# Two input chunk loads issued ahead of the constants, and the epilogue's f loads moved from GpSimd's queue to SyncE's

## The reference

```python
x = x + layernorm(attn(layernorm(x)))      # attn: LN, in_proj to 96, conv 3, silu,
                                           # selective scan (16 states), out_proj, + residual
x = x + layernorm(ffn(layernorm(x)))
def ffn(z):                                # router weight from a softmax over the top 2 of 8
    shared = (silu(z @ sh_gate.T) * (z @ sh_up.T)) @ sh_down.T      # 8192 wide
    routed = (silu(z @ r_gate.T) * (z @ r_up.T)) @ r_down.T         # 1024 wide
    return shared + routed * comb_w
```

## Time and profile before

| | |
|---|---|
| time, median of 3 runs | 2701.47 us (2700.31 to 2702.14) |
| the profiled execution's own time | 2702.35 us |
| its span (slowest core, core 7) | 2700.8 us |
| spans of the eight cores | 2684.7 to 2700.8 us |
| first TensorE instruction, core 7 | 24.83 us after the start |
| epilogue loop, from its first e1 to the end | 2569.16 to 2700.8 us |

### The profile page before, as it was taken

One profiled execution on the slowest core, in us unless ns is written; L12 is line 12 of the kernel. 1 busy time (PEld: TensorE's weight loads), 2 busy tenths in 40 slices (PEclk: granted clock), 3 DMA queues, 4 the chain that ended last, 5 costly groups with the idle time before them and its releaser, 6 DMA issues.

```text
span 2700.8 us, 27068 instructions; the slowest of 8 cores (2684.7 to 2700.8 us)
## 1 busy us (share of the span) xinstructions
PE 1921.2 (71%) x7719; PEld 779.8 (29%) x7719; DVE 396.1 (15%) x589; ACT 465.8 (17%) x802; POOL 363.7 (13%) x416
## 2 busy tenths in 40 slices
PE   4444543443323986899999999999979888888700
PEld 2111110000001432344444444444433333333300
DVE  0553343232363100000000000000000000000023
ACT  3333221231311112111111111111100000000100
POOL 1000000020200210122222222222200000000033
PEclk8655555555556989899999999999989999999855
DMA  6420001021132336444444444444434444344255
GB/s 100 59 32 0 0 0 62 1 78 48 44 121 55 63 67 152 78 79 78 77 74 74 75 78 79 79 79 78 76 66 92 94 94 90 84 92 94 55 187 179
DMA packets 67530, 203.23 MB, mean 75 GB/s; under 512 B 7420, under 2 KB 17789, under 8 KB 63302
## 3 DMA queue, kind: packets, MB, share of 16 engines
q0 software_dynamic: 40912, 132.88, 27.8%
q10 hardware_dynamic: 16128, 46.14, 4.6%
q1 hardware_dynamic: 10358, 22.48, 2.5%
HBM read 292.41 MB, written 33.55 MB: 121 GB/s over the span
## 4 chain that ended last, share of the span: by engine, by line
PE 66%; DVE 11%; DMA 8%; issue 7%; ACT 4%; POOL 2%; DVEq 0%; ACTq 0%; POOLq 0%; SPq 0%
PE pb L1120 16%; PE pb L1129 16%; PE pb L1174 5%; PE pb L1177 5%; PE pb L1189 4%; PE pb L1192 4%; DMA s_epf<-f_stash 2%; PE pb L1035 2%; PE pb L1044 2%; DVE s_xs L734 2%; PE pb L745 2%; DMA s_rdbuf<-Wrd 2%; POOL s_mr L858 2%; PE pb L1077 1%; DMA s_xhalf<-xT 1%
## 5 line engine op out<-in xcount | busy, mean ns | idle before, releaser
L1120 PE MATMUL pb<-s_z,s_gbuf 128*128 128x512 bf16 x2048 | 465.3, 380 | 13.6 <-issue 13.6
L1129 PE MATMUL pb<-s_z,s_ubuf 128*128 128x512 bf16 x2048 | 462.9, 379 | 0.0
L1120 PEld LDWEIGHTS pb<-s_z,s_gbuf 128*128 128x128 bf16 x2048 | 200.9, 98 | 257.4 <-issue 17.4
L1129 PEld LDWEIGHTS pb<-s_z,s_ubuf 128*128 128x128 bf16 x2048 | 200.4, 98 | 241.6
L1206 DVE TENSOR_TENSOR s_fstg<-pb,s_frbuf 128x512 f32<-128x512 f32 x32 | 20.6, 686 | 1545.2 <-PE pb L1192 1545.2
L1141 POOL TENSOR_TENSOR s_h<-s_gs,s_us 128x512 bf16<-128x512 bf16 x128 | 147.0, 1149 | 679.4 <-ACT s_us L1138 679.4
L1174 PE MATMUL pb<-s_h,s_dbuf 128*128 128x512 bf16 x512 | 209.6, 409 | 17.0 <-issue 16.6
L1177 PE MATMUL pb<-s_h,s_dbuf 128*128 128x512 bf16 x512 | 208.6, 407 | 0.0
L1189 PE MATMUL pb<-s_h,s_dbuf 128*128 128x512 bf16 x512 | 194.0, 379 | 4.1 <-PE pb L1177 4.1
L1192 PE MATMUL pb<-s_h,s_dbuf 128*128 128x512 bf16 x512 | 194.0, 379 | 0.0
L1135 ACT ACTIVATE s_gs<-pb 128x512 bf16<-128x512 f32 x128 | 76.4, 597 | 379.6 <-PE pb L1120 360.5
(11 more groups left out here) (193 smaller groups left out, 1479.9 us busy)
## 6 DMA issues: line engine op xcount, KB each, us to landing
s_gbuf<-Wg POOLq DMA_DIRECT2D x64, 512.0 KB, 5.2
s_ubuf<-Wu POOLq DMA_DIRECT2D x64, 512.0 KB, 7.1
s_dbuf<-Wd POOLq DMA_DIRECT2D x32, 1024.0 KB, 8.6
s_xcb<-xT POOLq DMA_DIRECT2D x5, 2048.0 KB, 18.1
s_xhalf<-xT SPq DMA_DIRECT2D x2, 4096.0 KB, 17.0
x_stash<-s_x2t ACTq DMA_DIRECT2D x32, 256.0 KB, 2.1
fr_stash<-s_frstg ACTq DMA_DIRECT2D x16, 512.0 KB, 5.4
s_frbuf<-fr_stash ACTq DMA_DIRECT2D x16, 512.0 KB, 7.7
```

The source lines that it names most:

```text
L1120: i2 = e.matmul(pb[bg][:, :], gbuf[ib][:, 128 * k:128 * (k + 1)], z4_sb[:, 1024 * k + hof:1024 * k + hof + 512], start=(k == 0), stop=(k = ...
L1129: i2 = e.matmul(pb[bu][:, :], ubuf[ib][:, 128 * k:128 * (k + 1)], z4_sb[:, 1024 * k + hof:1024 * k + hof + 512], start=(k == 0), stop=(k = ...
```

## The change

Two edits. `load_chunk` is defined earlier, and chunks 0 and 1 are issued by POOL ahead of its seven constants instead of behind them; the semaphores are dealt out anew by the rotation. In the epilogue, the f load is issued by SyncE instead of POOL, at the same place of the text, so that SyncE's list becomes f load 0, store 0, f load 1, store 1, and so on.

```diff
@@ prologue, behind the 16 loads of SyncE
+    x3 = xT.rearrange("(k p) t -> p k t", p=128)
+    t_xbf = [None] * NCHUNK
+    r_xcb_l = r_xcb
+
+    def load_chunk(c):
+        cc = c % 2
+        dst = xcb[cc].rearrange("p (k t) -> p k t", t=512)
+        t_xbf[c] = S.dma("gpsimd",
+                         lambda e, d=dst, c=c: e.dma_start(out=d,
+                                                           in_=x3[:, :, 512 * c:512 * (c + 1)]),
+                         writes=[r_xcb_l[cc]])
+
+    load_chunk(0)
+    load_chunk(1)
     for dst, src in [(outTbf, outT_h), (xprojTbf, xprojT_h), (dtprojTbf, dtprojT_h),
                      (selDbf, selD_h), (selBbf, selB_h), (selCbf, selC_h),
                      (routerTbf, routerT_h)]:
@@ mixer: the same lines removed here
-    load_chunk(0)
-    load_chunk(1)
@@ epilogue loop
-        t_lf = S.dma("gpsimd", lambda e, k=k, kk=kk: e.dma_start(
+        t_lf = S.dma("sync", lambda e, k=k, kk=kk: e.dma_start(
                          out=ep_f[kk][:], in_=f_st[k]), writes=[r_epf[kk]],
                      waits=[r_fst[k]])
```

## The result

The change made the kernel slower: 2768.47 us median against 2701.8 us, a ratio of 1.0247 (95% interval 1.0234 to 1.0259), or +66.7 us. The forecast was 2785 us, +83, in a range of 2748 to 2808. The profiled execution took 2766.97 us, its slowest core (core 2) spans 2765.4.

What follows compares the result with a forecast made beforehand. Only prologue (constants' consumers set the pace) and epilogue loop (a chain of waits) counted, the middle passing delays on. 2702.35 + 20.8 + 63.0 = 2786.2, median 0.9 lower: 2785 us predicted, 8-in-10 range 2748 to 2808.

Steps and rivals of the forecast that it cites:

- The prologue, +20.8: Kernel start: POOL's constants wait behind both chunk loads, so their consumers start at 45.6 us instead of 24.83.
- T1: Prologue: the time at which chunk 1 lands, put at 36.95 us.
- the rest behind it: Prologue after chunk 1: outT lands at 41.55, selB then routerT are issued, routerT lands 3.0 later, at 45.6 us.
- SyncE's constants cost nothing: Prologue: SyncE's 16 constants, in rounds of four, end at 33 us, before POOL's, so they add nothing.
- The f load leaves 5.69 us after e1: Epilogue loop: issued behind e3 and the store, the f load leaves 5.69 us after e1 instead of 3.67.
- It lands in 6.5: Epilogue loop: starting together with store and x2 load, the f load takes 6.5 us to land.
- the forecast's 63.0: Epilogue loop: 15 turns of 12.36 us instead of 8.16, +63.0 us.
- Rival A: Epilogue loop: f lands in about 4.5 us, not held by the store; turn 10.36, total 2755 us; chance 0.13.
- The tail at 0: Loop's end: the last e3 and store are as before, adding 0.
- Rival B: Prologue costs nothing: POOL's constants slip between the chunks' packets, only the loop is paid; 2764 us; chance 0.06.
- Rival C: Epilogue loop: SyncE's f loads run ahead of waiting stores, turn 5.2 us, -44; total 2678 us; chance 0.04.
- Rival D: Epilogue loop: SyncE's first byte comes sooner than GpSimd's, 0.6 against 1 us, 6 us lower; faster overall: chance under 0.01.

Runs made afterwards that it cites:

- edit-1 run: The kernel before with only chunks 0 and 1 moved ahead of POOL's constants, the f load left on POOL: 2724.02 us, ratio 1.0085.
- run without rotation: Chunks first, f load left on POOL; against that kernel, POOL's nine first DMAs got own semaphores, later instructions dropped waits for POOL's constants: 2679.7 us.
- e3: Not a run: the DVE instruction in each turn of the epilogue loop that the turn's store waits for; it takes 1.23 us.

## Why the prediction was right, and where its sizes were off

The sign and the mechanisms were right, the range held the time; one term was too large.

- *The prologue, +20.8.* Measured +21.4 on the mean of the cores, with the gaps and the order that were foretold. T1 was put at 36.95 and came at 39.2 to 42.2; the rest behind it was put at 8.7 us and took 5.8 to 6.8. Two errors that cancel: routerT took 2.0 and outT landed 1.4 us behind chunk 1, not 4.6. The edit-1 run confirms the whole, and the run without rotation shows that the semaphore waits, on which half of the argument rested, are 2 us of it. The order in POOL's queue, the other half, is the cause.
- *SyncE's constants cost nothing:* right. cconsts was issued at 24.77 on core 2 and landed 6.8 us later, and the last to land was routerT.
- *The f load leaves 5.69 us after e1:* 5.70 in the turn shown. Right.
- *It lands in 6.5:* this is the step that was mis-sized. I took the median of the store before and supposed that three transfers starting together would need the 7.5 us that they needed when one led. They needed 5.7, and f landed in 5.1 on core 2, 5.3 over all. 1.2 x 15 = 18 of the 19 us between the forecast's 63.0 and the 44.2 measured. The rows could not tell, since none had all three starting at once, but the trace before could have told more. At the start of its loop ACT issues the x2 loads of tiles 0, 1 and 2 within 0.9 us (2570.2 to 2571.1 on core 7), three 512 KB loads in one queue, and they land in

```profile
DMA to landing us min/median/max: 3.5/4.7/5.5
```

So the third, behind two others, takes 5.5 us and not 6.5. Rival A read the 3.5 of the first as that of a load that ran alone; it had two behind it. The run with the f load in SyncE's queue at the old moment shows that it was the old timing that made the others late, not the queue.
- *The tail at 0:* it was -1.1 us, from a cause that stays open.
- *By the rule on rings and packets* (the Trainium skill, "DMA: Bandwidth & Descriptors", "Queues, rings and completion order"), the store and the x2 load should share evenly and f follow the store. The trace agrees: store 4.5 and x2 load 4.6 after their issue, f 1.2 us behind the store. That alone does not show that f was late because of the shared queue: in the run with the late issue on POOL, f has a queue of its own and still lands last, 6.3 us after its issue where the others take 4.8 and 5.0.
- *Rival A* had f landing in about 4.5 and 2755 us; the measured 5.3 and 2768 us lie between it and the forecast. *Rival B* fell with the edit-1 run. *Rival C* did not occur, but its mechanism is real: with loads ahead of the stores a turn is 5.1 us, and the estimate for it was 5.2. *Rival D*, on the better queue, had the direction right: 0.24 us a landing in the run at the old moment, 1.0 us at the late one.
- *Two slips in the working.* In rival D the "4" of 4 + 20.8/15 stands for 4.2, by which the 5.6 comes out. The forecast's own range begins at 2762, where a landing of 5.5 (a turn of 11.36, +48) and a prologue of +15 give 2765. Neither changes the forecast.

Open: why the store and the x2 load take 6.1 to 6.4 us when an f load leads them by 1.4 us and 4.6 to 4.8 when it does not, why a POOL load lands 1 us later than one of SyncE in full company but only 0.24 us later otherwise, and what ends 1.1 us sooner behind the last e1.

## What to carry to other kernels

Before a DMA is moved to another engine's list, write down what stands ahead of it there and what that waits for: a load behind a store that waits for the end of the same turn's work can't run ahead. Put ahead of that store and two tiles early, in the same list, the load brought a turn from 11.1 us (8.1 before the change) to 5.1; put ahead of it but only as early as before, it brought 8.0. A large load issued ahead of small ones in POOL's queue holds them all up until it has landed, so what everyone waits for goes first, and each first instruction should wait for what it reads. Look for "issue" as the releaser ahead of TensorE's instructions: waits that are long since met are not free. What they cost is read from the stage's length without them, since another wait can take up the idle time that goes.

## What the runs showed of the hardware that I had not expected

- Eight met semaphore waits ahead of a matmul cost TensorE 0.39 us (32 matmuls, 12.5 us), four of them next to nothing (0.4 us over the 32), and taking such waits away everywhere gave 64 us, 2.3% of the kernel.
- Three 512 KB transfers that start together, with nothing else in flight, moved 350 GB/s and were done in 5.7 us; with one of them 1.4 us ahead, the other two took 6.1 to 6.4 us each, on whichever queue the first was.
- The same f load, issued at the end of e3 beside a store and a load, landed in 6.3 us from POOL and in 5.3 us from SyncE.
- In POOL's queue a load of 32 KB behind two chunk loads (8 MB read) landed 39.1 us after its issue, where in its old place it took 3.0.
